# Pairs of an expert's pages with one load of weights, and targets picked entry by entry

## What is computed

```python
logits = x @ router_w.T + expert_bias[None, :]
top_w, top_idx = jax.lax.top_k(jax.nn.sigmoid(logits), 8)      # of 160 experts
top_w = top_w / (sum(top_w) + 1e-9) * 2.5
h1 = silu(einsum('th,eih->eti', x, w_gate))                     # 256 -> 128
routed = einsum('eti,ehi->th', h1 * combine.T[:, :, None], w_down)
out = layernorm(x + routed + shared)
```

## Time and profile before

| what | us |
|---|---|
| median of 3 runs | 1020.51 (1018.35 to 1024.0) |
| the profiled execution | 1021.68 |
| its span | 1019.9 |
| first to last load of pages in `experts` | 588.15 to 938.33 |

### The profile page before, as it was taken

The page is one execution under the profiler, slowest core; times in us unless marked ns, Lnnn a source line. Parts: engine busy times, 40 slices in busy tenths (PEclk is TensorE's granted clock), DMA queues, the critical chain, the costliest instruction groups (busy, mean ns, idle before and its releaser), DMA issues. The chain is left out here.

```text
span 1019.9 us, 18292 instructions
## 1 busy us (share of the span) xinstructions
PE 818.2 (80%) x4178; PEld 543.9 (53%) x4178; DVE 509.4 (50%) x1400; ACT 445.7 (44%) x958; POOL 376.3 (37%) x376
## 2 busy tenths in 40 slices
PE   8999999999958989797960078787887877787495
PEld 4443333343334748474640066676776766676284
DVE  1677777877222475757565033343333334333066
ACT  2257776777724252516120034444445444454112
POOL 8000000000000003666677646566666666565200
PEclk9999999999987979998995579999999999999698
DMA  6998787785720102332225579999999999999595
GB/s 232 325 327 264 254 281 278 267 251 213 277 66 21 63 21 86 135 109 95 93 107 191 198 235 305 310 311 321 308 316 315 314 300 294 311 287 295 191 421 212
DMA packets 122058, 234.52 MB, mean 230 GB/s; under 512 B 29416, under 2 KB 61330, under 8 KB 115745
## 3 DMA queue, kind: packets, MB, share of 16 engines
q1 hardware_dynamic: 102720, 196.72, 58.3%
q0 software_dynamic: 17184, 35.20, 9.3%
q10 hardware_dynamic: 2112, 2.10, 0.6%
HBM read 142.80 MB, written 104.46 MB: 242 GB/s over the span
## 5 line engine op out<-in xcount | busy, mean ns | idle before, releaser
L1510 POOL DMA_INDIRECT contributions<-e_y,e_dest x230 | 223.8, 973 | 153.6 <-ACT e_y L1497 117.0
L1430 PE MATMUL e_psg<-e_xt,e_w 128*128 128x128 f32 x920 | 154.7, 294 | 76.9 <-DVE e_xt L1476 70.4
L1646 POOL DMA_INDIRECT row_pool<-rows,places x128 | 129.9, 1015 | 160.2 <-issue 136.3
L1430 PEld LDWEIGHTS e_psg<-e_xt,e_w 128*128 128x128 f32 x920 | 129.8, 204 | 87.7 <-DVE e_xt L1476 80.0
L1476 DVE COPY e_xt<-e_psx 128x256 f32<-128x256 f32 x230 | 97.4, 424 | 146.8 <-PE e_psx L1419 143.4
L497 DVE TENSOR_REDUCE a_mx<-a_psS 128x2 f32<-128x1024 f32 x128 | 152.0, 1218 | 32.7 <-PE a_psS L320 32.6
L455 ACT ACTIVATE a_e<-a_psT 128x512 f32<-128x512 f32 x256 | 138.0, 596 | 54.5 <-PE a_psT L350 52.2
L1490 ACT ACTIVATE e_g<-e_psg 128x128 f32<-128x128 f32 x230 | 63.7, 277 | 214.0 <-PE e_psg L1430 209.9
L1439 PE MATMUL e_psy<-e_w,e_g 128*128 128x256 f32 x460 | 147.5, 405 | 0.0
L1497 ACT ACTIVATE e_y<-e_psy,e_weight 128x256 f32<-128x256 f32 x230 | 108.9, 473 | 47.2 <-PE e_psy L1439 45.0
L1419 PE MATMUL e_psx<-c_ident,e_x 128*128 128x128 f32 x460 | 93.2, 287 | 45.1 <-DMA e_x<-row_pool 45.1
(11 more groups left out here) (214 smaller groups left out, 962.8 us busy)
## 6 DMA issues: line engine op xcount, KB each, us to landing
e_w<-w SPq DMA_DIRECT2D x230, 256.0 KB
row_pool<-fill SPq DMA_DIRECT2D x32, 1260.0 KB, 7.2
e_x<-row_pool SPq DMA_DIRECT2D x230, 140.0 KB
c_c<-contributions SPq DMA_DIRECT2D x16, 1024.0 KB, 15.2
a_k<-k_parts SPq DMA_DIRECT2D x64, 128.0 KB, 3.5
a_q<-q_parts SPq DMA_DIRECT2D x32, 128.0 KB, 4.0
a_q<-q_parts SPq DMA_DIRECT2D x64, 64.0 KB, 3.4
contributions<-e_y,e_dest POOLq DMA_INDIRECT x230
```

Source lines behind the costliest of these rows:

```text
L1430: last = nc.tensor.matmul(psG[:, f.k % 2, 0:n], W[:, f.slot, c * INTER:(c + 1) * INTER], XT[:, f.k % 2, c * n:(c + 1) * n], start=c == 0, ...
L1510: nc.gpsimd.indirect_dma_start(out=contrib, out_offset=bass.IndirectOffsetOnAxis(ap=dest[:, page(f) + k:page(f) + k + 1], axis=0), in_=Y[: ...
L1646: nc.gpsimd.indirect_dma_start(out=pool, out_offset=bass.IndirectOffsetOnAxis(ap=place[:, b, t, k:k + 1], axis=0), in_=rows[:, b, t], in_o ...
```

## The change

An expert's pages are taken in pairs: the entry of a pair loads the weights once and has two pages, side by side in the moving operand of the gate product (256 columns). A half now has seven entries, two pairs and five single pages (`PAIRED` sets their order), a body 14 entries with 18 pages. An expert with an odd number of pages gives its last one to the single entries, so every page is found by its number in the pool, and SyncE's list of a half has seven experts and nine pages, read with two loads. `list_entries` works out both lists; seven columns instead of three are spread by TensorE, and more columns are written by `fill_tables`. `pick` treats the pages of one entry, whole, behind the copy of its turned rows; the wait for all five loads is gone, ScalarE waits for its own entry's pick, and SyncE for the pick of the entry that had the slot. `BODIES` stays 32, so the loop still has 31 turns.

```diff
-FIRST, MORE = 3, 2
-ENTRIES = FIRST + MORE
-SLOTS = FIRST + MORE
-LISTED = 8
+PAIRS, ONES = 2, 5
+ENTRIES = PAIRS + ONES
+SLOTS = 2 * PAIRS + ONES
+PAIRED = (False, True, False, False, True, False, False)
+LISTED = 16
+PAGES = EXPERTS + UNITS
-PLACE_OF = COLUMN = (0, FIRST, 1, FIRST + 1, 2)
+COLUMN = tuple(sum(PAIRED[:j]) if PAIRED[j] else PAIRS + j - sum(PAIRED[:j]) for j in range(ENTRIES))
+PLACE_OF = tuple(2 * c if c < PAIRS else PAIRS + c for c in COLUMN)
...
-                    do(nc.vector.tensor_tensor_scan(firsts_to[:], ones_row[:], some[:], 0.0, ALU.mult, ALU.add))
-                    do(nc.vector.tensor_scalar(within[:], starts[:], at[:, 2:3], None, ALU.is_le))
-                    sync()
-                    do(nc.vector.scalar_tensor_tensor(within[:], ends[:], at[:, 2:3], within[:], ALU.is_le, ALU.subtract))
...
+                    do(nc.vector.tensor_tensor(low[:], starts[:], shifts[:], ALU.subtract))
+                    do(nc.vector.tensor_tensor(high[:], ends[:], shifts[:], ALU.subtract))
...
+                    do(nc.vector.scalar_tensor_tensor(pages_i[:], some[:], float(P), units_i[:], ALU.mult, ALU.add))
+                    do(nc.vector.tensor_tensor(last_shift[:], last_shift[:], moved[:], ALU.add))
+                    do(nc.vector.scalar_tensor_tensor(behind[:], units_i[:], 0.0, C[:, COL["expert"]], ALU.is_equal, ALU.mult))
...
+                    do(nc.vector.tensor_scalar(pairs_i[:], pages_i[:], 8, None, ALU.arith_shift_right))
+                    do(nc.vector.tensor_scalar(odds_i[:], pages_i[:], 7, 1, ALU.arith_shift_right, ALU.bitwise_and))
+                    do(nc.vector.tensor_tensor(last_page[:], units_i[:], last_shift[:], ALU.add))
...
+                    do(nc.vector.tensor_tensor(own[:], shifts[:], repeated(inside[:], 1, TT), ALU.mult))
+                    do(nc.vector.tensor_scalar(nth[:, 0:1], turn_of[:, 0:1], float(2 * P), float(-P), ALU.mult, ALU.add))
+                    do(nc.vector.tensor_scalar(nth[:, 1:2], turn_of[:, 0:1], float(2 * P), None, ALU.mult))
+                    do(nc.vector.tensor_scalar(turn_of[:, 1:2], turn_of[:, 0:1], 0.0, None, ALU.is_equal))
...
+                        for bound, found in ((low, opened), (high, closed)):
+                            do(nc.vector.scalar_tensor_tensor(scratch[:], bound[:], nth[:, i:i + 1], own[:], ALU.is_le, ALU.mult,
+                                                              accum_out=found[:, i:i + 1]))
+                            sync()
...
+                    for i in range(2):
+                        do(nc.vector.scalar_tensor_tensor(junk[:], odds_to[:], at[:, i:i + 1], ones_row[:], ALU.is_le, ALU.mult,
+                                                          accum_out=listed[:, 3 + i:4 + i]))
...
+                        do(nc.vector.scalar_tensor_tensor(junk[:], odds_from[:], at[:, i:i + 1], last_page[:], ALU.is_le, ALU.mult,
+                                                          accum_out=single[:, i:i + 1]))
+                        sync()
+                        do(nc.vector.scalar_tensor_tensor(junk[:], odds_to[:], at[:, i:i + 1], last_page[:], ALU.is_le, ALU.mult,
+                                                          accum_out=reach[:, i:i + 1]))
+                        sync()
...
+                    for i in range(7):
                         do(nc.vector.tensor_scalar(spread[:, i], ident, listed[:, i:i + 1], None, ALU.mult))
...
 
-    def half(self, h):
-
-        return self.nc.values_load_multi_w_load_instructions(
-            self.entry[0:1, bass.ds(h, 1)].rearrange("a h e -> a (h e)"), engines=[mybir.EngineType.SP], min_val=0,
-            max_val=EXPERTS, skip_runtime_bounds_check_because="every entry is an expert's number or the shared expert's")[1]
+    def half(self, h, pages=False):
+
+        load = lambda a, b, limit: self.nc.values_load_multi_w_load_instructions(
+            self.entry[0:1, bass.ds(h, 1), a:b].rearrange("a h e -> a (h e)"), engines=[mybir.EngineType.SP], min_val=0,
+            max_val=limit, skip_runtime_bounds_check_because="every entry is the number of an expert or of a page")[1]
+        return load(0, ENTRIES, EXPERTS), load(ENTRIES, LISTED, PAGES - 1) if pages else None
...
-            def load_rows(at, e):
-                n, j = pages(at), COLUMN[at_entry(at)]
-                row = e * P if j < FIRST else LATER + (at_half(at) * MORE + (j - FIRST)) * UNIT
-                sp.dma_start(X[:, page(at):page(at) + n],
-                             pool[bass.ds(row, n * P)].rearrange("(p k) r -> p k r", k=n)).then_inc(x_in[at.slot], 16)
+            def load_rows(at, listed_pages):
+                for k in range(pages(at)):
+                    number = listed_pages[PLACE_OF[at_entry(at)] + k]
+                    sp.dma_start(X[:, page(at) + k], pool[bass.ds(number * P, P)]).then_inc(x_in[at.slot], 16)
 
             def step(at):
                 h, j = half(at), at_entry(at)
                 if j == 0:
-                    listed[h] = tables.half(at_half(at))
-                v = listed[h][COLUMN[j]]
+                    listed[h] = tables.half(at_half(at), pages=True)
+                v = listed[h][0][COLUMN[j]]
                 if at.first(RING_E):
                     if at.n == 0:
                         sp.wait_ge(last_sent, 16 * TT * TOP_K)
-                    load_rows(at, v)
+                    load_rows(at, listed[h][1])
                     return
 
                 sp.wait_ge(turned, at.n - (RING_E - 1))
                 sp.sem_inc(x_loading, 1)
-                sp.wait_ge(picked, at_half(at) - (HALVES - 1))
+                sp.wait_ge(picked, at.n - (RING_E - 1))
                 sp.sem_inc(x_loading, 1)
-                load_rows(at, v)
+                load_rows(at, listed[h][1])
 
                 sp.wait_ge(downed, at.n - (RING_E - 1))
                 sp.sem_inc(w_loading, 1)
...
-                    pe.wait_ge(x_in[at.slot], 16 * at.uses())
+                    pe.wait_ge(x_in[at.slot], 16 * pages(at) * at.uses())
...
         def _(dve):
-            def pick(at, part):
-                h, hn = half(at), at_half(at)
-                slots = slice(h * SLOTS, (h + 1) * SLOTS)
-                if part == 0:
-                    for r in range(h * ENTRIES, (h + 1) * ENTRIES):
-                        dve.wait_ge(x_in[r], 16 * at.uses())
-                    nc.vector.tensor_tensor(same[:], X[:, slots, NAMES:ROW].bitcast(I32),
-                                            repeated(tables.expert[:, bass.ds(hn, 1)].rearrange("p h s -> p (h s)"), 2, TOP_K),
-                                            ALU.is_equal).then_inc(picking, 1)
-                if part == 1:
-                    dve.wait_ge(picking, hn * ORDERED + 1)
-                    nc.vector.tensor_tensor(chosen_w[:], X[:, slots, D:CODES], same[:], ALU.mult).then_inc(picking, 1)
-                    nc.vector.tensor_tensor(chosen_d[:], X[:, slots, CODES:NAMES], same[:],
-                                            ALU.mult).then_inc(picking, 1)
-                if part == 2:
-                    dve.wait_ge(picking, hn * ORDERED + 3)
-                    if not at.first(RING_E):
-
-                        dve.wait_ge(sent[h], 16 * SLOTS * (at.uses() - 1))
-                    nc.vector.tensor_reduce(weight[:, slots], chosen_w[:], AX, ALU.add).then_inc(picking, 1)
-                    nc.vector.tensor_reduce(slot[:], chosen_d[:], AX, ALU.add).then_inc(picking, 1)
-                    dve.wait_ge(picking, hn * ORDERED + 5)
-                    nc.vector.tensor_scalar(dest[:, slots], slot[:], BIG, None, ALU.add).then_inc(picked, 1)
+            def pick(at):
+
+                h, n = half(at), pages(at)
+                own = slice(page(at), page(at) + n)
+                of_page = tables.expert[:, bass.ds(at_half(at), 1), PLACE_OF[at_entry(at)]:PLACE_OF[at_entry(at)] + n]
+                nc.vector.tensor_tensor(same[:, 0:n], X[:, own, NAMES:ROW].bitcast(I32),
+                                        repeated(of_page.rearrange("p h s -> p (h s)"), 2, TOP_K),
+                                        ALU.is_equal).then_inc(picking, 1)
+                dve.wait_ge(picking, at.n * ORDERED + 1)
+                nc.vector.tensor_tensor(chosen_w[:, 0:n], X[:, own, D:CODES], same[:, 0:n], ALU.mult).then_inc(picking, 1)
+                nc.vector.tensor_tensor(chosen_d[:, 0:n], X[:, own, CODES:NAMES], same[:, 0:n], ALU.mult).then_inc(picking, 1)
+                dve.wait_ge(picking, at.n * ORDERED + 3)
+                if at_entry(at) == 0 and not at.first(RING_E):
+
+                    dve.wait_ge(sent[h], 16 * SLOTS * (at.uses() - 1))
+                nc.vector.tensor_reduce(weight[:, own], chosen_w[:, 0:n], AX, ALU.add).then_inc(picking, 1)
+                nc.vector.tensor_reduce(slot[:, 0:n], chosen_d[:, 0:n], AX, ALU.add).then_inc(picking, 1)
+                dve.wait_ge(picking, at.n * ORDERED + 5)
```

(44 more changed lines are left out.)

64 lines of the change are left out of this document (48 added, 16 removed).

## The result

The changed kernel takes 1034.17 us (median of 4 runs, 1031.49 to 1035.12) where the kernel before takes 1021.91 us (4 runs, 1018.35 to 1024.0): a ratio of 1.0119, 95% interval 1.0083 to 1.0156. It is **slower by 1.2%**; the forecast was 986 us. The profiled execution took 1034.28 us with a span of 1032.5 us, 12.6 us over the one before. The runs fall into batches, and in the batch of e1 to e4 every kernel, the one before too (1167.09 us), took some 147 us more than elsewhere, so its times are compared only with each other.

A forecast was written before the change was run, and what follows sets the result against it. SyncE's issuing was taken to set the pace, the DMA engines close behind. Terms of -50.2 + 4.6 + 2.4 (DMA share) + 3.0 + 7.3 - 1.5 = -34.4 us gave 986 us, range 974 to 1000.

The forecast's parts named there:

- Thirteen bodies: Expert loop: 52 pairs and 116 single pages fill 13 bodies instead of 23, with 182 weight loads and 234 page loads.
- rivals 2, 4 and 5: Expert loop: slots' wait starving GpSimd (1000 us, 0.09); VectorE's chain (1041 us, 0.04); picks holding GpSimd (1060 us, 0.02).
- the slots' wait: Expert loop: the wait for the slots' earlier use covers nine pages and costs nothing if transfers land within 11.5 us.
- Rival 1: Expert loop: the DMA engines set the pace before and after; 25.1 us a body, +3.6 us, 990 us; chance 0.22.
- the main term: SyncE's issuing in the expert loop: 24.6 us a new body, twelve bodies 295.2 us against 345.4, so -50.2 us.
- First body: Start of the expert loop: the first body issues 18 page loads in place of 10, +4.6 us.
- Start: Ahead of the expert loop: longer list work, later loads and slower scatters, together +3 us (bounds 0 and 8).
- the 594 us: Start of the expert loop: a first page load after 594 us would show the prediction wrong.
- End: After the last needed body: ten more empty turns on TensorE +7.3 us, the last half's shorter wait -1.5 us.
- the gain of the last half: End of the expert loop: the last half no longer waits for all its rows, -1.5 us.

The follow-up runs named there:

- e1: The changed kernel with twelve more SyncE list reads of 1 to 9, 12 and 16 values in idle time ahead of the tables; 1175.3 us in one run.
- e4: The kernel before with SyncE's list read twice per half, in the slow batch; 1182.24 us, ratio 1.0134 to the kernel before.
- e9: The kernel before with SyncE's list read twice per half, beside a kernel before of 1019.11 us; 1045.38 us, ratio 1.0243.
- e6: The changed kernel with a half's sixteen list values taken in one read from the row's start instead of two reads; 980.84 us, ratio 0.9644 to the kernel before.
- e7: The changed kernel with the page list moved from word 7 to word 8 of a 24-word row, still two reads; 998.81 us, ratio 0.9804 to the kernel before.
- e5: The changed kernel timed again, unaltered; 1032.84 us against 1019.83 for the kernel before, ratio 1.0131.
- e11: The changed kernel with its loop nested as 8 blocks of 4 turns, so unused blocks are passed whole; 1021.64 us, ratio 1.0022 to the kernel before.
- e12: The changed kernel with fourteen probe reads from various first words in SyncE's idle time; nine values took 0.91 to 1.03 us from words 0 and 4.
- e10: The kernel before with only the changed kernel's pick behind each entry's copy, with its waits; 1013.38 us against 1019.11, ratio 0.9942.
- e2: The changed kernel with its two list reads per half cut into four, of 4, 3, 5 and 4 values; 1180.77 us, ratio 1.0103 to the kernel before.

## Why the prediction was wrong

**What held.** Thirteen bodies: 182 loads of weights, 234 of pages. SyncE sets the pace without a wait of its own; e9 shows it of the kernel before, e6 of the changed one, where nothing but reads was taken from SyncE. An entry 1.33 us, a pair's second page 0.53 (0.57 was taken). Scatters 973 ns, VectorE's copy and pick 1.2 us for a page and 1.6 for a pair (from the copy's start to the target's end, medians from 600 to 900 us), the slots' wait 0.8 us in 300: rivals 2, 4 and 5 are out as causes. Rival 1 is out as the cause of the loss, since the share fell.

**The step that failed** is in the main term: "two more list reads, 0.53 us each with the register work and the gap, are +1.3 (bounds 1.1 to 2.4, since one read took 1.20 us)". It took the price of one read for reads of another shape. The 0.53 us are for eight values, a whole row of the kernel before; the changed kernel reads seven from word 0, and nine from word 7. Taken for a read of five, the read of before made seven look like a small step. Per half the reads are 0.94 + about 2.0 us where the term had 0.53 twice; the body came to 27.86 us, not 24.8. With the measured reads the prediction's own sum gives 24.6 + 2 x (2.97 - 0.53 - 0.65) = 28.2 us, so the rest of the term was sound. Twelve bodies: **+36.7 us** against the forecast. Both bounds came from rows for a read of another shape; the read that was new had no row at all, and its price has to be taken from a probe or kept open much wider. This alone turned a gain into a loss: with the page list one word further on (e7) the same change takes 998.8 us, inside the range, if at its upper end. That e6 (980.8 us) lies near the 986 of the forecast is in part luck, since it has one read a half where the forecast counted two.

**First body**: from the first page load to the end of the last weights are 943.83 - 595.70 = 348.1 us, of which twelve bodies are 334.3, so 13.8 are the first body's loads; before they were 5.7, and +4.6 was forecast. **+3.5 us**; the two lists of the second half are read in it as well.

**Start**: the first page load came at 595.70 us instead of 588.15, +7.5 where +3 was taken (within its bounds): **+4.5 us**. The 595.70 us are past the 594 us which the prediction named as a sign of being wrong. The lists took 17 us of VectorE (18 forecast). GpSimd's drain ended at 592.4 us, 6.2 us later than before, since the scatters ran later and two more of them took 1.5 and 1.6 us instead of 0.97; then comes the first pair of list reads. 2.9 us of it are there at the first instruction of the lists (541.98 against 539.13 us). In the other runs with this start the first page load came at 592.0 to 596.6 us (e5, e11, e12), so some of the 4.5 us is chance.

**End**: TensorE's pause grew from 6.04 to 13.27 us, +7.2 (7.3 forecast), and from the last weights to the first load of contributions the time grew from 21.8 to 27.7 us, +5.9 (5.8 forecast). e11 confirms the turns as a cost on the path. The difference, 1.3 us, is the gain of the last half (1.5 forecast); on the kernel before it was 2.9 us (e10). The last stage itself was 2.2 us longer, which was not in the sum.

Together: 36.7 + 3.5 + 4.5 + 0.1 + 2.2 = 47.0 us, and the forecast of -34.4 us becomes the +12.6 us of the two profiled executions.

**The range** was too narrow because both ends rested on the same rows as the middle. The slower rivals (4 and 5) looked for their trouble on the engines that get new work, and none asked what a new read costs on the queue that had just been named as the bound.

## What to carry to other kernels

Once a queue that only issues is the bound, a list read on it costs its whole length (e9: 44 reads, 26.3 us): count the reads as well as the DMAs, and price a read by its own size and place, with a probe in idle time if no row shows it. Take the size from the code that loads, not from the number of values that are used. Begin a list of indices at a multiple of four words, and read it in one piece: here one word of displacement cost 28 us in the loop and 34 of 1034 in all, and two reads instead of one another 18. A loop written for its worst case costs its empty turns at the end (0.73 us each on TensorE); nesting it in blocks takes most of that away.

## What was not expected of the hardware

What a read from SBUF into SyncE's registers costs hangs on where it begins and, in no steady order, on how many values it has. Nine values took 0.91 to 1.03 us from words 0 and 4, 0.74 us from word 8 (e7), and 2.0 to 2.6 us from five words that are no multiple of four (e12). Eight from the start of a row of eight took 0.53 us at the median in the loop of the kernel before, and four took 0.30 us (e2), while three from word 4 took 0.69 us (e2) and seven from word 0 took 0.94 us in the changed kernel. So eight are cheaper than seven, and four than three, in the loop as in the probes (e1: 0.69 against 1.09, and 0.72 against 1.09 us). Why, and whether a row padded to eight or sixteen values is always the better choice, is open.

The probes cost more than reads of the same shape in the loop: 0.72 against 0.30 us for four values, 0.69 against 0.53 for eight, 1.36 against 1.06 for sixteen (e6). They rank the shapes, but overstate what a read costs in the loop.
